# First slot tiles of a slot-attention kernel: from ScalarE and GpSimd passes to two VectorE operations per tile

## What is computed

```python
x_in = _ln(x, lnkv_g, lnkv_b)          # here x is the context, ctx_1024
k = x_in @ wk + bk
v = x_in @ wv + bv
slots = q_mu + jnp.exp(q_logsig) * noise   # here noise is _layernorm(x)
for _ in range(T):                         # T = 3 rounds
    q = _ln(slots, lnq_g, lnq_b) @ wq + bq
    ...                                    # attention over k, update, MLP
```

## Time and profile before

| | us |
|---|---|
| median of 3 runs (2638.29 to 2642.58) | 2639.43 |
| the profiled execution, its own time | 2632.51 |
| its span, first to last instruction | 2630.8 |
| PE busy | 2379.8 (90%) |
| DVE busy | 1614.4 (61%) |
| ACT busy | 979.8 (37%) |
| POOL busy | 1059.4 (40%) |
| granted PE clock, mean | 0.950 |

### The profile page before, as it was taken

One profiled execution on the slowest core, in us unless ns is written; L12 is line 12 of the kernel. 1 busy time (PEld: TensorE's weight loads), 2 busy tenths in 40 slices (PEclk: granted clock), 3 DMA queues, 4 the chain that ended last, 5 costly groups with the idle time before them and its releaser, 6 DMA issues.

```text
span 2630.8 us, 31285 instructions
## 1 busy us (share of the span) xinstructions
PE 2379.8 (90%) x11492; PEld 1926.3 (73%) x11492; DVE 1614.4 (61%) x2942; ACT 979.8 (37%) x1637; POOL 1059.4 (40%) x1520
## 2 busy tenths in 40 slices
PE   6988799999989999998999999899999556886997
PEld 3777688888878888877888887788888445654876
DVE  5777565657565675766576677657576665334532
ACT  1555433343334333333334333343334144445332
POOL 0555316161553536254443526363443573223100
PEclk9999899999999999999999999999999868777999
DMA  3576000000230000124000012400000222001330
GB/s 119 206 268 244 29 1 0 1 1 33 96 144 13 9 17 5 53 96 152 5 21 5 9 49 96 152 5 21 5 17 9 104 81 65 1 0 53 101 111 16
DMA packets 87247, 158.49 MB, mean 60 GB/s; under 512 B 12217, under 2 KB 34745, under 8 KB 84030
## 3 DMA queue, kind: packets, MB, share of 16 engines
q1 hardware_dynamic: 82710, 150.26, 16.4%
q0 software_dynamic: 2944, 6.31, 0.8%
q10 hardware_dynamic: 1450, 0.04, 0.0%
HBM read 106.21 MB, written 50.38 MB: 60 GB/s over the span
## 4 chain that ended last, share of the span: by engine, by line
PE 54%; DVE 20%; POOL 10%; issue 5%; ACT 5%; DMA 4%; SPq 0%; ACTq 0%; DVEq 0%; POOLq 0%
PE ps L204 17%; PE ps L206 16%; PE ps L205 16%; DVE moments L1399 4%; DMA ctx<-in_ctx_dram 2%; POOL gT1l L1933 2%; DVE mx L1698 2%; PE ps L970 2%; ACT prob L1315 2%; DVE zTl L1467 1%; DVE prob L1650 1%; DVE slots L1749 1%; DVE tbuf L1736 1%; POOL prb L708 1%; PE ps L964 1%
## 5 line engine op out<-in xcount | busy, mean ns | idle before, releaser
L204 PE MATMUL ps<-zTh,kTl 128*128 128x512 f32 (+1 forms) x912 | 336.3, 369 | 26.5 <-ACT prob L1315 22.5
L206 PE MATMUL ps<-zTh,kTh 128*128 128x512 f32 (+1 forms) x912 | 327.4, 359 | 0.0
L205 PE MATMUL ps<-zTl,kTh 128*128 128x512 f32 (+1 forms) x912 | 327.3, 359 | 0.0
L204 PE MATMUL ps<-vh,prob_lo 128*128 128x512 f32 x768 | 307.4, 400 | 11.5 <-DVE prob_lo L1680 11.5
L206 PE MATMUL ps<-vh,prob_hi 128*128 128x512 f32 x768 | 300.1, 391 | 0.0
L205 PE MATMUL ps<-vl,prob_hi 128*128 128x512 f32 x768 | 299.4, 390 | 0.0
L1467 DVE TENSOR_TENSOR zTl<-ps,zTh 128x512 fp32r<-128x512 f32 x224 | 151.1, 683 | 230.4 <-ACT zTh L1198 230.4
L1835 POOL TENSOR_SCALAR rs_m<-mv_m 128x1 f32<-128x1 f32 x96 | 39.4, 411 | 608.0 <-DVE mv_m L1401 606.0
L204 PEld LDWEIGHTS ps<-zTh,kTl 128*128 128x128 f32 x912 | 174.0, 191 | 60.7 <-ACT prob L1315 26.2
L1315 ACT ACTIVATE prob<-ps,nb 128x1024 f32<-128x1024 f32 x96 | 107.3, 1118 | 295.9 <-DVE nb L1703 295.9
L1180 ACT ACTIVATE zbuf<-slots,rs_m 128x512 f32<-128x512 f32 x96 | 78.4, 816 | 344.3 <-POOL rs_m L1839 344.3
(11 more groups left out here) (298 smaller groups left out, 5794.7 us busy)
## 6 DMA issues: line engine op xcount, KB each, us to landing
ctx<-in_ctx_dram SPq DMA_DIRECT2D x8, 1024.0 KB, 11.4
slots<-in_x_dram SPq DMA_DIRECT2D x8, 1024.0 KB, 11.6
stg<-in_x_dram SPq DMA_DIRECT2D x8, 1024.0 KB, 10.1
x_d<-stg SPq DMA_DIRECT2D x8, 1024.0 KB, 6.2
kT_d<-kTh SPq DMA_DIRECT2D x6, 1024.0 KB, 4.7
kT_d<-kTl SPq DMA_DIRECT2D x6, 1024.0 KB, 6.7
s_d<-slots SPq DMA_DIRECT2D x6, 1024.0 KB, 4.4
v_d<-vh SPq DMA_DIRECT2D x6, 1024.0 KB, 6.4
```

The costliest lines, as they stand in the source:

```text
L204: nc.tensor.matmul(out, ll, rh, start=start, stop=False)
L205: nc.tensor.matmul(out, lh, rl, start=False, stop=False)
L206: return nc.tensor.matmul(out, lh, rh, start=False, stop=stop)
```

## The change

For all eight passes, the ACT step `x_norm` and the two POOL steps of `first_slots` go. In their place DVE has, for each tile, one operation (x - m) * row 0, and one operation * r + row 1, each adding one to `si_step`. POOL's `rstd_x` keeps its first two operations (variance + eps, and the power) and drops the two that made -m*r. In DVE's queue of passes 0 to 6, tile 0 stands before `v_in(h, 4)`, tile 1 before `v_in(h, 5)`, tile 2 behind `c_lo(h + 1, 3)`, and tile 3 behind `kv_lo(h, 7)`, the last `kv_lo` of the pass. In pass 7, tiles 0 and 1 stand behind `kv_lo(7, 1)`, tiles 2 and 3 behind `kv_lo(7, 3)`. The order of everything else is as before.

```diff
@@ -1216,11 +1216,6 @@
                 dst = kT[0][:, u, cut(nh, 512)] if u < 4 else v[0][:, 4 * nh + u - 4, :]
                 A.activation(dst, g, ACT.Copy).then_inc(sem("kv_hi"), 1)
 
-            def x_norm(h, i):
-                j = 4 * (h % 2) + i
-                act.wait_ge(sem("nm_x"), 4 * (h + 1))
-                normalize("x", slots[:, j, :], slots[:, j, :], j).then_inc(sem("x_normed"), 1)
-
             def z_normalize(yc, j):
                 g = yc // NT
                 if j >= 2:
@@ -1248,15 +1243,12 @@
                 kv_hi(h, 1)
                 c_norm(h + 1, 3); c_hi(h + 1, 1)
                 kv_hi(h, 2)
-                x_norm(h, 0)
                 kv_hi(h, 3)
-                x_norm(h, 1); c_hi(h + 1, 2)
+                c_hi(h + 1, 2)
                 kv_hi(h, 4)
-                x_norm(h, 2)
                 kv_hi(h, 5)
                 c_hi(h + 1, 3)
                 kv_hi(h, 6)
-                x_norm(h, 3)
                 kv_hi(h, 7)
                 if h == 5:
                     act.wait_ge(sem("w1_scaled"), C)
@@ -1264,9 +1256,7 @@
 
             h = HS - 1
             kv_hi(h, 0)
-            x_norm(h, 0); x_norm(h, 1)
             kv_hi(h, 1)
-            x_norm(h, 2); x_norm(h, 3)
             kv_hi(h, 2)
             act.wait_ge(sem("wst_c"), 2 * 16)
             A.activation(w2[0][:, :, :], wst["w2f"][:, :, :], ACT.Copy).then_inc(sem("w_hi"), 1)
@@ -1500,6 +1490,16 @@
                 dve.wait_ge(sem(f"x_in{h % 2}"), (h // 2 + 1) * 16)
                 stats("x", 4 * h + i, j, slots[:, j, :])
 
+            def first_slots(h, i):
+                j = 4 * (h % 2) + i
+                s_ = slots[:, j, :]
+                V.scalar_tensor_tensor(s_, s_, mv["x"][:, j, 0:1], rows[:, 0, :], ALU.subtract, ALU.mult)\
+                    .then_inc(sem("si_step"), 1)
+                dve.wait_ge(sem("si_step"), 8 * h + 2 * i + 1)
+                dve.wait_ge(sem("nm_x"), 2 * (h + 1))
+                V.scalar_tensor_tensor(s_, s_, rs["x"][:, j, 0:1], rows[:, 1, :], ALU.mult, ALU.add)\
+                    .then_inc(sem("si_step"), 1)
+
             def z0_stats(h, i):
                 j = 4 * (h % 2) + i
                 dve.wait_ge(sem("si_step"), 8 * h + 2 * i + 2)
@@ -1527,22 +1527,26 @@
                 kv_lo(h, 3)
                 dot_m(h + 1, 2)
                 c_lo(h + 1, 2)
+                first_slots(h, 0)
                 v_in(h, 4)
                 if more:
                     c_stats(h + 2, 1)
                 kv_lo(h, 4)
                 dot_m(h + 1, 3)
+                first_slots(h, 1)
                 v_in(h, 5)
                 if more:
                     c_stats(h + 2, 2)
                 kv_lo(h, 5)
                 c_lo(h + 1, 3)
+                first_slots(h, 2)
                 if more:
                     c_stats(h + 2, 3)
                 v_in(h, 6)
                 kv_lo(h, 6)
                 v_in(h, 7)
                 kv_lo(h, 7)
+                first_slots(h, 3)
                 if h == 6:
                     dve.wait_ge(sem("w_hi"), 1)
                     V.tensor_tensor(w1[1][:, :, :], wst["w1f"][:, :, :], w1[0][:, :, :].bitcast(f32), ALU.subtract)\
@@ -1554,6 +1558,7 @@
             for i in range(4):
                 z0_stats(h - 1, i)
             kv_lo(h, 1)
+            first_slots(h, 0); first_slots(h, 1)
             dve.wait_ge(sem("craw_ready"), 4 * HS)
             V.tensor_scalar(cr[:, :, :], craw[:, :, :], c0[:, 0:1], LOGIT_SCALE, ALU.add, ALU.mult)\
                 .then_inc(sem("craw_ready"), 1)
@@ -1562,6 +1567,7 @@
             V.tensor_tensor(w2[1][:, :, :], wst["w2f"][:, :, :], w2[0][:, :, :].bitcast(f32), ALU.subtract)\
                 .then_inc(sem("w_split"), 1)
             kv_lo(h, 3)
+            first_slots(h, 2); first_slots(h, 3)
             v_in(h, 4); kv_lo(h, 4); z_lo(0, 0)
             v_in(h, 5); kv_lo(h, 5); z_lo(0, 1)
             for i in range(4):
@@ -1855,17 +1861,16 @@
                 rstd_four("c", "nm_c", h, mv["c"][:, cut(h % 2, 4), :], rs["c"][:, cut(h % 2, 4), :])
 
             def rstd_x(h):
-                rstd_four("x", "nm_x", h, mv["x"][:, cut(h % 2, 4), :], rs["x"][:, cut(h % 2, 4), :])
+
+                j = cut(h % 2, 4)
+                pool.wait_ge(sem("mv_x"), 8 * h + 8)
+                G.tensor_scalar(rs["x"][:, j, 1:2], mv["x"][:, j, 1:2], LN_EPS, None, ALU.add).then_inc(sem("nm_x"), 1)
+                pool.wait_ge(sem("nm_x"), 2 * h + 1)
+                G.tensor_tensor(rs["x"][:, j, 0:1], rs["x"][:, j, 1:2],
+                                minus_half[:, :].rearrange("p (k o) -> p k o", o=1), ALU.pow).then_inc(sem("nm_x"), 1)
 
             def rstd_z0(h):
                 rstd_four("z", "nm_z0", h % 2, mv["z"][:, cut(h % 2, 4), :], rz0[:, cut(h % 2, 4), :])
-
-            def first_slots(h, i):
-                j = 4 * (h % 2) + i
-                pool.wait_ge(sem("x_normed"), 4 * h + i + 1)
-                G.tensor_tensor(slots[:, j, :], slots[:, j, :], rows[:, 0, :], ALU.mult).then_inc(sem("si_step"), 1)
-                pool.wait_ge(sem("si_step"), 8 * h + 2 * i + 1)
-                G.tensor_tensor(slots[:, j, :], slots[:, j, :], rows[:, 1, :], ALU.add).then_inc(sem("si_step"), 1)
 
             def scale_w1(c):
 
@@ -1879,13 +1884,10 @@
             pool.wait_ge(sem("rows_in"), 5 * 16)
             for h in range(HS):
                 rstd_x(h)
-                first_slots(h, 0)
                 if h == HS - 1:
                     rstd_z0(h - 1)
-                first_slots(h, 1); first_slots(h, 2)
                 if h + 2 < HS:
                     rstd_c(h + 2)
-                first_slots(h, 3)
                 if 1 <= h <= C:
                     scale_w1(h - 1)
             rstd_z0(HS - 1)
```

## The result

The changed kernel takes **2656.6 us** (median of 4 runs, 2653.9 to 2659.6) against 2638.9 for the kernel before beside it: a ratio of 1.0065, 95% interval 1.0049 to 1.0081, so 17.7 us slower, with 13 to 21 in the interval. The forecast was 2653.9, +14.5, in a range of 2646 to 2662. The profiled execution took 2655.8 us, span 2654.1.

A forecast was written before the change was run, and what follows sets the result against it. A prologue loop of waits through the context load, DVE's tail and SP's slots store was taken as the bound. Terms +1.2, +1.1, +12.8, +1.5, -1.6 and rounding -0.5 gave +14.5 on 2639.4: 2653.9 us, range 2646 to 2662.

The forecast's parts named there:

- The loop: Prologue pass, store to store: tail (context landing to SP's slots store) plus store to next landing; +3.2 us a turn.
- Price of a tile: DVE's two new operations per tile in the prologue: 0.77 and 0.63, together 1.4 us; new tail 18.3 us.
- Pass 0: First prologue pass, where nothing waits for a load: SP's slots store comes 1.2 us later.
- Pass 1: Second prologue pass: its tail of 17.2 us becomes 18.3, +1.1 us.
- Passes 2 to 5: Four prologue turns, each 3.2 us longer: +12.8 us.
- the transfers are the same: Prologue transfers, context loads included: the same ones in the same order, counted at nothing.
- Passes 6 and 7: End of the prologue: +1.5 us in pass 6, -1.6 in pass 7, rounding -0.5; slot rounds start 14.5 us later.
- POOL's relief: Prologue DVE operations with two SBUF inputs, no longer held up by POOL's removed passes: 1.0 us back in pass 3.
- POOL's one-input work blocking DVE: Rival, prologue tails: POOL's remaining operations block DVE too, 2 to 7 us more, 2658.6 us; 10%.
- The fused operations at twice the pace: Rival, DVE's new prologue operations: 0.3 to 0.4 us each, 2634.4 us at 0.76 a tile; 3%.
- A sooner landing: Rival, prologue context loads: landing 2 us sooner in each of five turns, 2643.9 us; 6%.
- PE as the limit: Rival, prologue: PE at half clock for a whole pass, +8 us in each of five turns, 2694 us; 2%.

The follow-up runs named there:

- one operation per tile: The changed kernel with the second DVE operation of each tile left out (first adds two to `si_step`): 2634.4 us, ratio 0.9988.
- two tiles in ACT waits: The changed kernel with tile 2 moved before `kv_lo(h, 6)` and tile 3 before `kv_lo(h, 7)`, where DVE waits for ACT: 2639.7 us, ratio 1.0003.
- POOL's passes kept: The changed kernel with POOL's 64 passes over 512 columns kept as idle work into an unused tile: 2687.6 us, ratio 1.0186.
- the early load: Context load moved ahead of SP's wait for `si_step`: changed kernel 2635.5 us (0.9985); kernel before 2627.0 us (0.9951), repeated 2629.1 us (0.9964).

## Why the prediction was right

**The loop.** Where the context load still ends DVE's wait, a turn is the tail plus the time from the store's issue to the next landing, and only the tail moves:

| kernel | tail, us | turn, us | rest of the turn |
|---|---|---|---|
| before | 15.1 | 28.6 | 13.5 |
| one operation per tile | 15.4 | 28.8 | 13.4 |
| two tiles in ACT waits | 16.4 | 29.6 | 13.2 |
| changed | 18.5 | 32.0 | 13.5 |
| POOL's passes kept | 22.1 | 35.6 | 13.5 |

The tail is that of one turn of each profile, the turn the mean of four. As the tail grows by 7 us, the rest of the turn stays within 0.3. That is the theory of the forecast in its plainest form. That it is the order of SP's queue which closes the loop is shown by the early load, which took DVE's 24.0 us of waiting away with no other edit.

**Price of a tile.** Forecast 1.4 us from start to start, measured 1.45 (the first operation to the second 0.78, the second to the next 0.67). Tail forecast 18.3, measured 18.5. This term was mis-sized by 0.2 us a turn, 1.0 in all.

**Pass 0.** Forecast +1.2; from the first input load to the store 35.25 before and 36.54 after, +1.3.

**Pass 1.** Forecast +1.1, measured 33.11 - 30.28 = +2.8. The tail gave 1.3 (18.5 where it was 17.2); the other 1.6 is the landing, 12.6 us from the issue of the context load where it had been 11.0. This is the largest single miss of this execution; in the repeat of the changed kernel the same landing took 12.0. **Passes 2 to 5**: forecast +12.8, measured +13.7: 0.9 more, most of it the 0.2 a turn. The step "the transfers are the same" put landings at no change; over five passes they come to 57.0 us before, 58.6 after, and 57.8 in the repeat of the changed kernel. With single landings of 10.9 to 12.6 us within one execution, whether the change lengthens them by 1 us in all is not settled.

**Passes 6 and 7.** Measured 62.8 us from the last store to the first product, where it was 63.2: -0.4. Split at the end of w1's low half on DVE it is +1.35 and -1.8, where the forecast had +1.5 and -1.6: both terms hold. The forecast's own -0.6 does not follow from them, though. 15.1 + 1.5 - 1.6 is 15.0, and the further "-0.5" for rounding that leads to 14.5 is worked out from nothing.

**The sum.** 1.3 + 2.8 + 13.7 - 0.4 = 17.4 against 14.5; against the 15.0 of the forecast's own terms the miss is 2.4 us, nearly all of it in the landing of pass 1 (1.6) and in the tails (1.0). After the prologue nothing changed that can be told from scatter.

**What POOL's relief is worth.** The forecast had DVE get back 1.0 us a tail. The new profile has no lengthened operation left, and the run with POOL's passes kept shows that they do cost time. With all 64 of both kinds the kernel is slower than with either alone. What a split, some tiles on POOL and some on DVE, would cost was not run.

**Rivals.** POOL's one-input work blocking DVE: no. In the turn shown above L1878 ran from 200.16 for 1.57 us and `kv_lo` started inside it at 201.09 and took 0.69:

```profile
200.16 1.57 POOL L1878 TENSOR_SCALAR st_w1f<-st_w1f,columns 128x512 f32<-128x512 f32 x1
```

That is the case which the rule of the Trainium skill (SBUF — State Buffer, "SBUF: two separate sides") would have blocked. By that rule any GpSimd operation that reads SBUF excludes a two-input VectorE operation; by these rows the two-input POOL passes do, and this one-input operation does not, in any of the four passes that have it, before or after the change. The fused operations at twice the pace: no, 745 and 752 ns. A sooner landing: no, if anything later. PE as the limit: no, though it came nearer than the forecast had it. PE's wait for `c_lo` in that turn grew from 2.33 us to 4.93. The granted clock over the window of pass 3 was 0.89 where it had been 1.00, and behind that wait the matmuls started 0.43 us apart in place of 0.23, for some 5 us, where the forecast had allowed for 3. The turn had room for both: at the transposes PE still waited 0.72 us, where it had waited 1.75.

```profile
195.60 0.80 PE L204 MATMUL ps<-zTh,m1l 128*128 128x512 f32 x1 [4.93 <-DVE zTl L1457]
...
201.81 0.66 PE L970 MATMUL ps<-ident,zc 128*128 128x128 f32 x4 [0.72 <-ACT zc L1180]
```

The price of that rival was too low as well: at 0.43 in place of 0.23 us a matmul, 24.9 us would become some 46, not 40.

The profile's chain that ended last could not be used here: for this execution it reaches back only to 2080 us, the last 22% of the span. The distances of stores and DVE's idle time before its statistics gave the answer instead.

## What to carry to other kernels

Before moving work to an engine that is busy for 60% of the time, find the wait that starts its idle time and put the work on the near side of it, or into short waits for another engine's answer: against the kernel before, and with POOL's relief counted in, the same 64 operations cost 17.7 us behind the landing, about nothing with half of them in two waits of 0.7 us, and went with a gain of 6 us when the other half stood ahead of the landing. Look also at what a store's wait holds up in an in-order queue; here the larger gain, 9 to 13 us on the kernel before (ratios 0.9964 and 0.9951), lay in letting the next load pass it, and it needed no compute change at all. No order of the changed kernel that was run came below that; the best, 0.9968, lies within its scatter. Free time is not one pool, though: filling the wait for the load entirely closed another loop, over PE and ACT, only 3.5 us a turn shorter than the first.

## What the runs showed of the hardware that was not expected

A DVE operation with two SBUF inputs that meets a POOL operation with two inputs of 512 columns loses up to about a microsecond (0.69 to 1.70, 0.75 to 1.77), and in a queue with many of both it adds up: 31 us for 64 passes nobody waits for. POOL's one-input operation on the same columns did not do it to `kv_lo`. In `pool_passes_kept`, though, in each of its four passes, it took 2.00 us itself and the DVE operation that started inside it 1.06 in place of 0.75, so the two are not wholly blind to each other; what decides there stays open.
